# Query and key splits stacked by three transfers instead of row copies, with the four heads of a block side by side

## The chip, the cores and the metric

One Trainium2 chip, one of its cores. The metric is device time in microseconds of one execution of the whole program, lower is better. Profiles are single executions; line numbers such as L930 are lines of the kernel before.

## The reference

Input `x` has 8 batches of 512 tokens and 512 channels; a context of 77 tokens per batch has a length of its own per batch. Two residual steps follow each other, both with 16 heads of 32 channels:

```python
x = x + cross_attention(layernorm(x), ctx, ctx, valid_lens, Wq, Wk, Wv, Wo)   # keys past valid_lens masked
h = layernorm(x)
top_idx, gates = top_2(relu(mean(h) @ gw1.T + gb1) @ gw2.T + gb2)             # per batch, of 8 experts
q, k, v = (h @ (Wm + sum_k gate_k U_k S_k V_k).T + b for each of q, k, v)
x = x + self_attention(q, k, v) @ (Wm_o + ...).T + ob                         # softmax over 512 keys
```

Everything is float32. Scores are exponentiated after the row maximum is subtracted.

## The kernel before

The work of each batch `b` is cut into some 480 small steps (kinds such as `qk`, `sc`, `sT`, `pv`). A table, `CALENDAR`, gives each step of a batch a number, to which `b * PERIOD` is added; batches 0 and 7 and a few steps of batch 6 have numbers of their own in `OWN`. All steps are sorted by these numbers, and every engine, and SP's DMA queue, walks the sorted list and does the steps that are its own, in that order. The numbers have no other use: what counts is the order. Between engines, steps wait on semaphores. Six batches in the middle repeat one order, and neighbouring batches overlap: while batch 3 is in its self attention, batch 4 is in its cross attention.

Heads come in four jobs of four (`j`, or `i` in the cross attention): 128 columns of a projection hold four heads of 32 channels.

- `q1` and `qk` (through `product`, L1236) project a job's queries or keys into a bank of PSUM, 128 rows (head, channel) by 512 tokens, with float32 matmuls; each is recorded as two MATMULs. `out1`, `v` and `out2` are products of the same size.
- `q1_split`, `qk_split`: ScalarE writes the rounded high part to `stage_hi` (L898, L905), VectorE the remainder to `stage_lo` (L1048, L1055). There are three stage buffers. The float32r matmuls that follow take one pass each.
- The stack: a tile `qs`, `ks` or `qsc` of 32 rows per part, three parts on top of each other (high, high, low for queries; high, low, high for keys), the four heads side by side in columns, so that one matmul of 96 rows sums three products. Each of `qs` and `ks` has two slots (`j % 2`).
- `q1_rows`, `qk_rows`: ScalarE copies each head's 32 rows of `stage_hi` to part 0 of the stack: four ACTIVATE of 32 x 512 (L916, L930). `q1_stack`, `qk_stack`: SP issues four transfers of 64 KB from `stage_lo` to the low part (L692, L708), waits for the row copies, and issues one of 256 KB that copies part 0 to the other high part (L695, L711).
- `csc`, `sc` (L1282, L1293): scores, in two banks; VectorE takes the row maxima (L1064, L1072). `cross_shift`, `shift`: TensorE transposes the maxima (L1299), VectorE splits them (L1079, L1081), and `shift_move` (L747) moves them by two transfers of 8 KB into two more rows of the query stack. `csT`, `sT` (L1314, L1321): transposed scores with the maximum subtracted; ScalarE exponentiates them (L938, L949).
- `pv`, `den`, `cpv`, `cden`: four heads beside each other, eight MATMULs. `psum` (GpSimd) adds the exponentials over key tiles; `inv` takes reciprocals, `divide` scales.
- The gate of the next batch (`gate_hidden`, `gate_top`, `gate_scale`, `pick`, `uv_load`, `uv_hi`, `uv_lo`, `weff`) runs beside it: SP reads the chosen experts (`pick`) and loads their factors (`uv_load`) and the plain weights (`wm_load`, L727); `weff` (L1266) multiplies the factors, and VectorE adds the result to the plain weights (L1159).

The PSUM banks for products (`pj`, three) and the stage buffers are handed out in the sorted order, so the order also sets which step waits for which bank.

Of the kernel before, what the change touches and what calls it, by code (L numbers as in the profile page):

```python
# [16 lines left out]
H, DH = 16, 32  # L17
# [25 lines left out]
PERIOD = 32544  # L43
CALENDAR = {
    "context": (-29527,),
    "context_v": (-22528,),
    "load": (-32665,),
    "stats": (-32183, -31868, -31599, -31477),
    "deviation": (-30034, 295),
    "normalize": (-28685, 1275),  # L50
    "xpose": (-27589, -27427, -26822, -26780, 1562, 1957, 2590, 2902),
    "q1": (-26590, -26243, -25959, -25937, -26536, -25485, -24792, -24419, -18087, -17907, -17456, -16554, -12209,
        -12014, -11705, -11434),
    "q1_split": (-25157, -24232, -15571, -10200),
    "q1_rows": (-24756, -18383, -13331, -7974),
    "q1_stack": (-24276, -17659, -11767, -7302),
    "pick": (4904,),
    "uv_load": (5886, 6812, 9234, 43415),
    "csc": (-23802, -23433, -22705, -22506, -16659, -16588, -16069, -15948, -11709, -11333, -10125, -9654, -5344,
        -5090, -4931, -4819),  # L60
    "cross_shift": (-22083, -15813, -9063, -4218),
    "cross_shift_move": (-21652, -15771, -8769, -4153),
    "csT": (-20791, -20067, -19513, -19512, -14418, -14247, -13713, -13489, -8539, -8329, -8228, -8041, -3571, -3381,
        -3091, -3068),
    "cpv": (-18262, -10397, -6973, -2567),
    "cacc": (-18190, -10093, -6231, -2378),
# [12 lines left out]
    "uv_hi": (5956, 8589, 9867, 47462),
    "uv_lo": (6039, 8816, 10639, 49210),  # L80
    "weff": (6968, 7223, 8095, 8162, 9130, 9401, 9822, 9845, 10725, 10762, 12444, 12542, 53344, 53841, 53973, 55499),
    "qk": (8248, 8472, 8477, 8636, 9921, 10045, 10194, 10492, 17793, 18105, 19037, 19131, 19533, 19591, 19715, 19966,
        22679, 22995, 23492, 24077, 24628, 26820, 27705, 27722, 33581, 33788, 33991, 34872, 36496, 36571, 36871, 37170),
    "qk_split": (8792, 11460, 19921, 20217, 24193, 27804, 35667, 37980),
    "qk_rows": (12829, 12428, 21163, 21940, 28716, 28090, 37032, 38667),
    "qk_stack": (14166, 13070, 21170, 23206, 29374, 29180, 38577, 39510),
    "v": (11539, 12230, 12965, 13658, 12386, 12506, 12605, 14080, 14702, 15911, 16094, 16166, 16257, 16627, 16862,
        18707),
    "v_bias": (14155, 14210, 16179, 19056),
# [5 lines left out]
    "shift": (20612, 29950, 38368, 45601),  # L95
    "shift_move": (22291, 30030, 38966, 46828),
# [36 lines left out]
    "weff": {(7, 3, 0): 322347, (7, 3, 1): 329712, (7, 3, 2): 371975, (7, 3, 3): 389041, (0, 0, 0): 7543,
# [14 lines left out]
    "load": {(0,): -877946},  # L148
    "stats": {(0, 0): -446619, (0, 1): -446600, (0, 2): -446546, (0, 3): -435175},
# [180 lines left out]
def increments(step):  # L330
# [1098 lines left out]
```

## Time and profile before

| | |
|---|---|
| median of 3 runs | 1408.98 us (1406.68 to 1409.2) |
| the profiled execution | 1410.16 us, span of the trace 1408.4 us, TensorE clock 0.995 |
| TensorE matmuls | 1370.0 us busy (97%), 5704 instructions |
| weight loads | 690.0 us (49%) |
| VectorE, ScalarE, GpSimd | 948.3 us (67%), 857.2 us (61%), 679.7 us (48%) |
| DMA | 130.81 MB, mean 93 GB/s |

A row of the trace gives start and length of an instruction, or how often it came, and the idle time of its engine before it with the one that ended that. Ends of matmuls are modelled: several are in the pipeline at once, so rows overlap, and the length of one row is not the time that TensorE spends on it. The chain of waits shows what each added to the end.

### The profile page before, as it was taken

Reading aid. Unit: us, or ns where it says so; the run is one execution under the profiler, and the core shown is the slowest. Engines: PE = TensorE matmul, PEld = TensorE weight load, DVE = VectorE, ACT = ScalarE, POOL = GpSimd, SP = SyncE. Lnnn points to the kernel's source line nnn. Section 1 sums busy time; section 2 is a strip of 40 time slices with the busy share of each in tenths; the row PEclk is TensorE's granted clock in tenths of the full one; section 3 lists DMA queues with packets and bytes.
Section 4 is the critical chain, followed back from the end, with each engine's and each line's share of the span. In section 5 each row is a group of like instructions: output and inputs, shape, how many; then the busy total and the mean of one; then the engine's idle time right before and its main releaser. Section 6 shows DMA issues by size and latency. Waiting matters only on the chain.

```text
span 1408.4 us, 17104 instructions
## 1 busy us (share of the span) xinstructions
PE 1370.0 (97%) x5704; PEld 690.0 (49%) x5704; DVE 948.3 (67%) x1679; ACT 857.2 (61%) x1499; POOL 679.7 (48%) x411
## 2 busy tenths in 40 slices
PE   8999999999999999999999999999999999999987
PEld 5545445544455554554455544555544444444432
DVE  3573677767677776767677676767776667676573
ACT  2435566766488655866567654885558655585562
POOL 2023045554457543564556543575535545575485
PEclk9999999999999999999999999999999999999999
DMA  7443224423344213622244323442145222342311
GB/s 255 97 141 103 64 51 120 126 59 86 113 97 111 65 50 111 161 49 77 75 119 119 76 62 113 99 116 67 41 134 140 47 77 64 94 114 65 81 41 37
DMA packets 78767, 130.81 MB, mean 93 GB/s; under 512 B 26374, under 2 KB 32134, under 8 KB 75607
## 3 DMA queue, kind: packets, MB, share of 16 engines
q1 hardware_dynamic: 78103, 129.61, 34.6%
q8 instruction: 45, 0.74, 0.2%
q14 instruction: 43, 0.35, 0.1%
q10 hardware_dynamic: 576, 0.11, 0.1%
HBM read 66.08 MB, written 12.21 MB: 56 GB/s over the span
## 4 chain that ended last, share of the span: by engine, by line
PE 80%; ACT 5%; DVE 4%; DMA 4%; SPq 3%; issue 2%; POOL 1%; DVEq 0%; ACTq 0%; POOLq 0%
PE pj L1236 41%; PE scT L1321 8%; PE sc L1293 8%; PE acc L1350 7%; PE sc L1282 3%; PE pj L1266 2%; PE scT L1314 2%; PE pj L1338 2%; PE pj L1330 2%; PE pj L1359 1%; SPq L708 1%; PE pj L1209 1%; DVE inv_sum L1099 1%; DVE negmax L1072 1%; PE pj L1221 1%
## 5 line engine op out<-in xcount | busy, mean ns | idle before, releaser
L949 ACT ACTIVATE probs<-scT 128x512 f32<-128x512 f32 x512 | 289.5, 594 | 298.8 <-PE scT L1321 295.2
L1072 DVE TENSOR_REDUCE negmax<-sc 128x1 f32<-128x512 f32 x512 | 339.5, 681 | 151.1 <-PE sc L1293 148.3
L821 POOL TENSOR_TENSOR probs_sum<-probs_sum,probs 128x1024 f32<-128x1024 f32 x128 | 300.5, 2366 | 67.6 <-ACT probs L949 67.5
L1099 DVE RECIPROCAL inv_sum<-pj 128x128 f32<-128x128 f32 x256 | 225.7, 923 | 69.9 <-PE pj L1359 38.5
L817 POOL TENSOR_TENSOR probs_sum<-probs 128x1024 f32<-128x1024 f32 x64 | 151.2, 2369 | 247.7 <-ACT probs L949 247.7
L1321 PE MATMUL scT<-qs,ks 99*128 99x512 f32 x512 | 258.8, 541 | 10.4 <-DMA qs<-shift 5.3
L1293 PE MATMUL sc<-ks,qs 96*128 96x512 f32 x512 | 258.2, 532 | 3.5 <-DVE negmax L1072 1.8
L1236 PE MATMUL pj<-XT,Wqk 128*128 128x512 f32 x512 | 257.8, 595 | 0.0
L1321 PEld LDWEIGHTS scT<-qs,ks 99*128 99x128 f32 x512 | 94.0, 189 | 118.5 <-ACT probs L949 47.2
L1293 PEld LDWEIGHTS sc<-ks,qs 96*128 96x128 f32 x512 | 96.3, 189 | 111.3 <-issue 62.5
L1350 PE MATMUL acc<-probs,V 128*32 128x512 f32 x1024 | 132.2, 600 | 0.0
L1236 PE MATMUL pj<-Wvo,ctx2T 128*128 128x512 f32 x256 | 129.6, 598 | 0.2 <-DVE inv_sum L1099 0.2
L1236 PE MATMUL pj<-Wvo,XT 128*128 128x512 f32 x256 | 128.2, 599 | 0.2 <-DVE V L1170 0.2
L791 POOL TENSOR_TENSOR xhat<-xhat,inv_sum 128x128 f32<-128x128 f32 (+1 forms) x56 | 45.7, 820 | 170.6 <-DVE inv_sum L1099 116.6
L938 ACT ACTIVATE probs<-scT 77x512 f32<-77x512 f32 x128 | 71.2, 586 | 91.0 <-PE scT L1314 90.0
L1236 PE MATMUL pj<-XT,Wq_sb 128*128 128x512 f32 x256 | 126.2, 605 | 0.0
L1236 PE MATMUL pj<-Wo_sb,xhat 128*128 128x512 f32 x256 | 121.4, 596 | 0.0
L827 POOL TENSOR_TENSOR uv_stack<-UVS_sb,uv_stack 96x1024 fp32r<-96x1024 f32 x32 | 75.6, 2363 | 85.6 <-ACT UVS_sb L869 85.6
L1236 PEld LDWEIGHTS pj<-XT,Wqk 128*128 128x128 f32 x512 | 94.8, 190 | 45.2 <-issue 24.9
L1282 PEld LDWEIGHTS sc<-keys,qsc 97*128 97x128 f32 x480 | 69.6, 192 | 42.3 <-issue 28.3
L1282 PE MATMUL sc<-keys,qsc 97*128 97x78 f32 x480 | 82.8, 303 | 4.5 <-DMA qsc<-qsc 2.7
L1064 DVE TENSOR_REDUCE negmax<-sc 128x4 f32<-128x312 f32 x128 | 60.2, 475 | 33.1 <-PE sc L1282 32.9
(102 smaller groups left out, 1722.7 us busy)
## 6 DMA issues: line engine op xcount, KB each, us to landing
Wqk<-in_WmT SPq DMA_DIRECT2D x16, 1024.0 KB, 6.6
Wvo<-in_WmT SPq DMA_DIRECT2D x16, 1024.0 KB, 5.8
UVS_sb<-in_UVS SPq DMA_DIRECT2D x64, 192.8 KB, 3.2
qs<-stage_lo SPq DMA_DIRECT2D x136, 64.0 KB, 2.1
qs<-qs SPq DMA_DIRECT2D x34, 256.0 KB, 3.0
X<-in_x SPq DMA_DIRECT2D x8, 1024.0 KB, 8.1
ks<-stage_lo SPq DMA_DIRECT2D x128, 64.0 KB, 2.0
ks<-ks SPq DMA_DIRECT2D x32, 256.0 KB, 2.9
```

The costliest lines, as they stand in the source:

```text
L817: nc.gpsimd.tensor_tensor(probs_sum[:, pair], probs[:, 0, pair], probs[:, 1, pair], ALU.add)\
L821: nc.gpsimd.tensor_tensor(probs_sum[:, pair], probs_sum[:, pair], probs[:, kt % 2, pair], ALU.add)\
L827: nc.gpsimd.tensor_tensor(uv_stack[:].rearrange("p s n -> p (s n)"), UVS_sb[:, n, 0:2 * D], uv_stack[:].rearrange("p s n -> p (s n)").bitc ...
L938: nc.scalar.activation(probs1[0:NK, j, :], scT[0:NK, ST[step], :], ACT.Exp, scale=SCALE)\
L949: nc.scalar.activation(probs[:, kt % 2, jj, :], scT[:, ST[step], :], ACT.Exp, scale=SCALE)\
L1072: nc.vector.tensor_reduce(negmax[:, 0, n:n + 1], sc[:, SC[step], :], AX.X, ALU.max, negate=True)\
L1099: nc.vector.reciprocal(inv_sum[:, INV[use], at], pj[:, PJ[left_in(full)], at])\
L1236: mm = nc.tensor.matmul(pj[:, p, :], lhsT, rhs, start=(dc == 0), stop=(dc == DC - 1))
L1282: mm = nc.tensor.matmul(sc[:, SC[step], j * NKP:(j + 1) * NKP], cross_stack(b, i)[0:MASK_ROW + 1, j, t * P:(t + 1) * P], keys1[0:MASK_ROW ...
L1293: nc.tensor.matmul(sc[:, SC[step], :], qs[0:3 * DH, slot, jj, t * P:(t + 1) * P], ks[0:3 * DH, slot, jj, :], start=True, stop=True).then_i ...
L1321: nc.tensor.matmul(scT[:, ST[step], :], ks[0:ROWS, slot, jj, kt * P:(kt + 1) * P], qs[0:ROWS, slot, jj, :], start=True, stop=True).then_in ...
L1350: mm = nc.tensor.matmul(acc[jj * DH:(jj + 1) * DH, 0, :], V2[:, kt, v_slot(b, j), jj * DH:(jj + 1) * DH], probs[:, kt % 2, jj, :], start=( ...
```

## The change

The columns of the first query weight, and the output columns of the query and key weights and of their biases, are permuted on the host: within each block of 128, row `d * 4 + head` takes the place of row `head * 32 + d`. A split of 128 partitions by 512 is then, in order, 32 rows by four heads by 512, as the stack wants it. ScalarE's row copies are gone. SP issues three transfers of 256 KB per split, each from 128 rows of a stage buffer to 32 rows of the stack: two of the high part once ScalarE has written it, one of the low part once VectorE has. The waits that the row copies had (the slot is free, the constant rows are made) are SP's now. Nothing else in the computation changes; the numbers of all steps are new, in sixteenths of the old unit (520704 = 16 x 32544), those of batches 0 and 7 too.

```diff
-PERIOD = 32544
+PERIOD = 520704
 CALENDAR = {
-    "pick": (4904,),
-    "uv_load": (5886, 6812, 9234, 43415),
+    "pick": (69426,),
+    "uv_load": (76373, 89903, 137903, 683234),
...
-    "wm_load": (2594, 8306, -276, 53109),
+    "wm_load": (60219, 116462, 54068, 827809),
...
-    "gate_scale": (5530,),
+    "gate_scale": (80616,),
...
-    "qk_split": (8792, 11460, 19921, 20217, 24193, 27804, 35667, 37980),
-    "qk_rows": (12829, 12428, 21163, 21940, 28716, 28090, 37032, 38667),
-    "qk_stack": (14166, 13070, 21170, 23206, 29374, 29180, 38577, 39510),
...
-    "shift": (20612, 29950, 38368, 45601),
-    "shift_move": (22291, 30030, 38966, 46828),
...
+    "qk_stack": (212732, 185553, 342481, 374955, 491818, 480494, 603756, 608930),
...
+    "shift": (342227, 479168, 605178, 724794),
...
-    if kind in ("q1_rows", "qk_rows"):
-        return {"rows_copied": HJ}
     if kind == "q1_stack":
-        return {f"q1_stacked{home_of(*step[1:])}": 16 * (HJ + 1)}
+        return {f"q1_stacked{home_of(*step[1:])}": 16 * 3}
...
+            def stacked(stack, parts, n, split, done):
+                sp.wait_ge("stage_hi", sp.after("stage_hi", *split))
+                for part in parts[:2]:
+                    queue.dma_start(stack[part * DH:(part + 1) * DH].bitcast(F32), stage_hi[:, n, :].bitcast(F32))\
+                         .then_inc(done, 16)
+                sp.wait_ge("pj_left_by_dve", sp.after("pj_left_by_dve", *split))
+                queue.dma_start(stack[parts[2] * DH:(parts[2] + 1) * DH].bitcast(F32), stage_lo[:, n, :].bitcast(F32))\
+                     .then_inc(done, 16)
...
             def qk_stack(step, b, j, w):
                 split = "qk_split", b, j, w
-                n, slot = STAGE[split], slot_of(j)
-                stack, lo, hi = ((qs, 2, 1), (ks, 1, 2))[w]
-                sp.wait_ge("pj_left_by_dve", sp.after("pj_left_by_dve", *split))
+                slot, (stack, parts) = slot_of(j), ((qs, (0, 1, 2)), (ks, (0, 2, 1)))[w]
+                sp.wait_ge("consts_made", 7)
+                sp.wait_ge("ks_made", sp.after("ks_made", "key_rows", 1))
...
-                for jj in range(HJ):
-                    queue.dma_start(stack[lo * DH:(lo + 1) * DH, slot, jj, :].bitcast(F32),
-                                    stage_lo[jj * DH:(jj + 1) * DH, n, :].bitcast(F32)).then_inc(done, 16)
-                sp.wait_ge("rows_copied", sp.after("rows_copied", "qk_rows", b, j, w))
-                queue.dma_start(stack[hi * DH:(hi + 1) * DH, slot].bitcast(F32),
-                                stack[0:DH, slot].bitcast(F32)).then_inc(done, 16)
+                stacked(stack[:, slot], parts, STAGE[split], split, sems[f"{'qk'[w]}_stacked{slot}"])
...
-            def qk_rows(step, b, j, w):
-                slot, stack = slot_of(j), (qs, ks)[w]
...
-                for jj in range(HJ):
-                    nc.scalar.activation(stack[0:DH, slot, jj, :], stage_hi[jj * DH:(jj + 1) * DH, n, :].bitcast(F32),
-                                         ACT.Copy).then_inc(sems["rows_copied"], 1)
...
+    def by_row(a):
+        return np.asarray(a).reshape(*a.shape[:-1], DC, HJ, DH).swapaxes(-1, -2).reshape(a.shape)
```

In the new table `shift_move` has (346303, 481205, 606551, 734915), `qk_split` (126830, 171885, 314027, 318477, 394952, 472792, 569878, 607147).

## Rows read from the trace of the kernel before

**Rows 1.** Busy time by stretch: length, busy of each engine, clock, DMA share, GB/s.

```profile
0.00:220.00 220.00, 207.69 (x840) 112.01 (x840) 127.06 (x230) 103.31 (x175) 50.20 (x45) 0.98 0.43 123
220.00:1060.00 840.00, 833.67 (x3542) 424.01 (x3540) 597.22 (x1074) 546.69 (x963) 432.14 (x259) 1.00 0.36 92
1060.00:1240.00 180.00, 172.94 (x733) 85.40 (x732) 122.96 (x219) 115.67 (x205) 89.11 (x51) 1.00 0.33 85
1240.00:1408.40 168.40, 155.66 (x595) 68.57 (x593) 101.10 (x158) 91.56 (x160) 108.24 (x57) 0.99 0.24 65
```

**Rows 2.** Chain in order of time, 600 to 660 us: start, us, what.

```profile
608.91 1.72 PE pj L1236 x4
621.54 0.46 PE scT L1321 x2
624.20 0.37 PE sc L1282 x4
635.37 0.86 PE acc L1350 x8
```

**Rows 3.** Timeline of TensorE: the gate's matmuls of two neighbouring batches.

```profile
564.67 1.11 PE L1368 MATMUL pj<-pooled,gw1T_sb 128*128 128x128 f32 x8
728.04 1.12 PE L1368 MATMUL pj<-pooled,gw1T_sb 128*128 128x128 f32 x8
```

**Rows 4.** Groups of ScalarE by shape: count, busy us, mean ns, idle before.

```profile
L949 ACT ACTIVATE probs<-scT 128x512 f32<-128x512 f32 x512 | 289.5, 594 | 298.8 <-PE scT L1321 295.2 <-POOL probs_sum L817 1.3
L930 ACT ACTIVATE qs<-stage_hi 32x512 fp32r<-32x512 f32 x128 | 80.2, 627 | 2.7
```

**Rows 5.** Waits of TensorE's matmuls: us in total, times, longest.

```profile
PE scT L1321 <- DMA qs<-shift: 5.3, 8, 1.1
PE scT L1321 <- ACT probs L949: 3.4, 8, 0.5
...
PE sc L1282 <- DMA qsc<-qsc: 2.7, 2, 2.3
...
PE pj L1299 <- DVE stage_lo L1055: 1.6, 6, 0.3
```

**Rows 6.** Timeline, 731 to 762 us, around the end of job 2 of one batch.

```profile
733.23 2.58 ACT L930 ACTIVATE qs<-stage_hi 32x512 fp32r<-32x512 f32 x4
...
736.79 0.69 ACT L905 ACTIVATE stage_hi<-pj,qkb_sb 128x512 fp32r<-128x512 f32 x1
737.23 2.47 SPq L708 DMA_DIRECT2D qs<-stage_lo  x4
...
737.51 0.75 DVE L1055 SCALAR_TENSOR_TENSOR stage_lo<-pj,qkb_sb,stage_hi 128x512 fp32r<-128x512 f32 x1 [0.76 <-ACT stage_hi L905]
...
738.32 0.33 PE L1299 MATMUL pj<-ident_sb,negmax 128*128 128x128 f32 x1 [0.28 <-DVE stage_lo L1055]
...
740.38 1.23 SPq L747 DMA_DIRECT2D qs<-shift  x2
743.71 0.72 PE L1321 MATMUL scT<-qs,ks 99*128 99x512 f32 x2 [0.44 <-DMA qs<-shift]
...
752.98 0.58 SPq L727 DMA_DIRECT2D Wqk<-in_WmT  x1
...
760.00 1.28 DVE L1159 TENSOR_TENSOR Wqk<-pj,Wqk 128x512 f32<-128x512 f32 x2
```

**Rows 7.** DMA issues: count, KB each, us from issue to landing.

```profile
Wqk<-in_WmT SPq DMA_DIRECT2D x16, 1024.0 KB, 6.6
...
qs<-stage_lo SPq DMA_DIRECT2D x136, 64.0 KB, 2.1
qs<-qs SPq DMA_DIRECT2D x34, 256.0 KB, 3.0
...
ks<-ks SPq DMA_DIRECT2D x32, 256.0 KB, 2.9
...
qs<-shift SPq DMA_DIRECT2D x68, 8.0 KB, 2.4
```

More of the change, by code:

```diff
@@ new lines @@
+    "q1_stack": (-415245, -291066, -204261, -115894),
+    "pick": (69426,),
+    "uv_load": (76373, 89903, 137903, 683234),
+    "csc": (-399316, -392329, -386570, -361778, -279999, -267576, -262032, -259985, -181121, -174415, -153549,
+        -151999, -89000, -80879, -77224, -70003),
+    "cross_shift": (-357091, -258799, -145893, -61252),
+    "cross_shift_move": (-338882, -252460, -145637, -58247),
+    "csT": (-326112, -321104, -317390, -311544, -246868, -243436, -227048, -223831, -139203, -137355, -130085,
+        -128804, -42655, -42231, -39567, -39079),
@@ new lines @@
+    "cpv": (-282558, -158643, -117491, -36343),
+    "cacc": (-270843, -158024, -104649, -32670),
+    "cden": (-255862, -167520, -106954, -35308),
+    "cinv": (-253918, -250906, -245859, -223367, -163757, -161195, -160591, -155900, -104782, -84249, -77203, -76914,
+        -34463, -32438, -29645, -18601),
+    "wm_load": (60219, 116462, 54068, 827809),
+    "cdivide": (-161540, -148848, -47603, -28681, -11770, -8982, 1170),
+    "out1": (-50162, -44668, -40472, -14842, -27878, -27789, -23527, -9127, -9100, -6339, -2183, 5204, 3938, 6459,
+        6628, 10929),
@@ new lines @@
+    "residual1": (-8176, -1589, 9151, 13278),
+    "residual_bias": (298894,),
+    "token_sums": (32668, 44433, 48684, 49029),
+    "gate_hidden": (60147,),
+    "gate_top": (64114,),
+    "gate_scale": (80616,),
+    "uv_hi": (87261, 111461, 147491, 738169),
+    "uv_lo": (87300, 123017, 165328, 822345),
+    "weff": (101588, 107032, 109352, 111400, 128962, 137507, 140208, 147209, 174882, 175894, 178873, 189936, 850122,
+        864319, 867823, 898426),
+    "qk": (113828, 114593, 114952, 120109, 149163, 160907, 163385, 164241, 276060, 278903, 295107, 299779, 300581,
+        301097, 313751, 314218, 369736, 375334, 377029, 379567, 437349, 440750, 445804, 457938, 532516, 543784,
+        544129, 548328, 576496, 580646, 585989, 590801),
@@ new lines @@
+    "qk_split": (126830, 171885, 314027, 318477, 394952, 472792, 569878, 607147),
+    "qk_stack": (212732, 185553, 342481, 374955, 491818, 480494, 603756, 608930),
+    "v": (188740, 196964, 208643, 226468, 211931, 212863, 214459, 229455, 252723, 255436, 260811, 262576, 268470,
+        272012, 272014, 282674),
+    "v_bias": (229466, 234781, 264193, 287174),
[5 rows of a table added]
+    "shift": (342227, 479168, 605178, 724794),
+    "shift_move": (346303, 481205, 606551, 734915),
[7 rows of a table added]
+    "psum": (380589, 403679, 419958, 444044, 444527, 464186, 537796, 545354, 577378, 578721, 592602, 597747, 647186,
+        659111, 675085, 696260, 698722, 751132, 782551, 790720, 849174, 868486, 878058, 881981),
@@ new lines @@
+    "accout": (520658, 610322, 747005, 897008),
+    "den": (476400, 607559, 758606, 884123),
+    "inv": (476548, 479438, 480346, 481164, 612511, 612537, 613577, 614055, 761956, 763020, 777076, 782945, 889711,
+        894768, 901184, 902009),
+    "divide": (533142, 705594, 850295, 903864, 905126, 909312, 970769),
+    "out2": (902822, 903802, 906599, 916862, 913457, 914464, 916922, 917886, 938998, 939278, 949506, 957981, 967566,
+        971705, 976463, 989555),
+    "residual2": (918189, 918352, 959695, 989800),
@@ L207 @@
-    "gate_hidden": {(0,): 4930, (7,): 231575},
-    "gate_top": {(0,): 5490, (7,): 231738},
-    "gate_scale": {(0,): 5710, (7,): 232050},
-    "pick": {(0,): 5670, (7,): 232919},
-    "warm": {(0, 2): -96451, (1, 3): -47401, (2, 1): -40402, (3, 4): -29966, (4, 5): -24131, (5, 2): -3041,
-        (6, 3): 3898, (7, 3): 4589, (8, 2): 8768, (9, 3): 9592, (10, 4): 11483},
-    "residual_bias": {(7,): 242974},
[7 rows of a table removed]
-    "qk_split": {(7, 0, 0): 236698, (7, 0, 1): 238528, (7, 1, 0): 248314, (7, 1, 1): 249344, (7, 2, 0): 267927,
-        (7, 2, 1): 266852, (7, 3, 0): 310186, (7, 3, 1): 321828},
@@ new lines @@
+    "context": {(0,): -4192709},
+    "context_v": {(0,): -1151284, (7,): 3296262},
+    "wm_load": {(7, 3): 5049208, (0, 0): -555476, (0, 1): -545137, (0, 2): 127050, (7, 1): 3743833, (7, 0): 3684340,
+        (7, 2): 3648630},
+    "uv_load": {(7, 3): 3873399, (0, 0): 85489, (0, 1): 104189, (0, 2): 122536, (7, 2): 3738706, (7, 0): 3705733,
+        (7, 1): 3726657},
+    "uv_hi": {(7, 3): 4774211, (0, 0): 87401, (0, 1): 113882, (0, 2): 157228, (7, 1): 3740283, (7, 2): 3791436,
+        (7, 0): 3721389},
@@ new lines @@
+    "uv_lo": {(7, 3): 5310646, (0, 0): 98804, (0, 1): 118690, (0, 2): 176485, (7, 1): 3764726, (7, 2): 3818370,
+        (7, 0): 3732600},
+    "weff": {(7, 3, 0): 5311761, (7, 3, 1): 5312059, (7, 3, 2): 5445882, (7, 3, 3): 6767537, (0, 0, 0): 99661,
[14 rows of a table added]
+    "load": {(0,): -15904755},
+    "stats": {(0, 0): -15845340, (0, 1): -15844419, (0, 2): -15838204, (0, 3): -9167904},
+    "deviation": {(0, 0): -9159449, (0, 1): 16037, (7, 1): 3652060},
+    "normalize": {(0, 0): -6602126, (0, 1): 19582, (7, 1): 3671415},
@@ new lines @@
+    "csT": {(0, 0, 0): -1199395, (0, 0, 1): -1199186, (0, 0, 2): -1181853, (0, 0, 3): -1180673, (0, 1, 0): -1132007,
[5 rows of a table added]
+    "cpv": {(0, 0): -1142434, (0, 1): -732056, (0, 2): -648967, (0, 3): -80188, (7, 0): 3392474, (7, 1): 3445833,
+        (7, 2): 3528428, (7, 3): 3609282},
+    "cacc": {(0, 0): -1121586, (0, 1): -720649, (0, 2): -83537, (0, 3): -79327, (7, 0): 3393471, (7, 1): 3448477,
+        (7, 2): 3533095, (7, 3): 3609477},
+    "cden": {(0, 0): -1148189, (0, 1): -1046493, (0, 2): -664387, (0, 3): -544673, (7, 0): 3389423, (7, 1): 3473974,
+        (7, 2): 3537267, (7, 3): 3611764},
@@ new lines @@
+    "cinv": {(0, 0, 0): -1132201, (0, 0, 1): -1129012, (0, 0, 2): -1117869, (0, 0, 3): -736503, (0, 1, 0): -727355,
[6 rows of a table added]
+    "cdivide": {(0, 0, 0): -718118, (0, 1, 0): -583452, (0, 2, 0): -80738, (0, 3, 0): -78635, (0, 3, 1): -64755,
[11 rows of a table added]
+    "token_sums": {(0, 0): 49688, (0, 1): 65308, (0, 2): 68626, (0, 3): 68706, (7, 0): 3676931, (7, 1): 3686265,
+        (7, 2): 3686524, (7, 3): 3691101},
+    "gate_hidden": {(0,): 68746, (7,): 3695798},
+    "gate_top": {(0,): 74895, (7,): 3696637},
+    "gate_scale": {(0,): 76550, (7,): 3699359},
@@ new lines @@
+    "pick": {(0,): 76841, (7,): 3700382},
+    "warm": {(0, 2): -4194136, (1, 3): -3603782, (2, 1): -3595382, (3, 4): -1057802, (4, 5): 55759, (5, 2): 68223,
+        (6, 3): 68968, (7, 3): 89527, (8, 2): 129061, (9, 3): 171381, (10, 4): 406600},
+    "residual_bias": {(7,): 3736107},
[8 rows of a table added]
+    "qk_split": {(7, 0, 0): 3759505, (7, 0, 1): 3829138, (7, 1, 0): 3976891, (7, 1, 1): 3989439, (7, 2, 0): 4414129,
+        (7, 2, 1): 4411404, (7, 3, 0): 5117183, (7, 3, 1): 5438284},
+    "qk_stack": {(7, 0, 0): 3823567, (7, 0, 1): 3841901, (7, 1, 0): 4006334, (7, 1, 1): 4027510, (7, 2, 0): 4467432,
[5 rows of a table added]
@@ new lines @@
+    "v_bias": {(7, 0): 3873002, (7, 1): 3874231, (7, 2): 3909227, (7, 3): 3957891},
[13 rows of a table added]
+    "shift": {(7, 0): 3981117, (7, 1): 4452327, (7, 2): 5310973, (7, 3): 6705351},
+    "shift_move": {(7, 0): 4007764, (7, 1): 4468990, (7, 2): 5313784, (7, 3): 6745515},
[20 rows of a table added]
+    "psum": {(7, 0, 1, 0): 4128274, (7, 0, 1, 1): 4409351, (7, 0, 2, 0): 4427773, (7, 0, 2, 1): 4432218,
[5 rows of a table added]
+    "accout": {(7, 0): 4813425, (7, 1): 5440670, (7, 2): 6823813, (7, 3): 14056979},
+    "den": {(7, 0): 4765132, (7, 1): 5446756, (7, 2): 6820617, (7, 3): 14053237},
@@ L290 @@
            "normalize": product(PAIR), "xpose": product(PAIR, FOUR), "q1": product(JOBS, FOUR),
-           "q1_split": product(JOBS), "q1_rows": product(JOBS), "q1_stack": product(JOBS),
+           "q1_split": product(JOBS), "q1_stack": product(JOBS),
            "pick": [()], "uv_load": product(FOUR), "csc": product(JOBS, FOUR), "cross_shift": product(JOBS),
@@ L297 @@
            "weff": product(FOUR, FOUR), "qk": product(JOBS, PAIR, FOUR), "qk_split": product(JOBS, PAIR),
-           "qk_rows": product(JOBS, PAIR), "qk_stack": product(JOBS, PAIR), "v": product(FOUR, FOUR),
+           "qk_stack": product(JOBS, PAIR), "v": product(FOUR, FOUR),
            "v_bias": product(FOUR), "sc": product(JOBS, range(TT * HJ)), "shift": product(JOBS),
@@ L906, in qk_split @@
                                      bias=qkb_sb[:, w, j:j + 1]).then_inc(sems["stage_hi"], 1)
-            def q1_rows(step, b, i):
-                before = home_before(b, i)
-                act.wait_ge("consts_made", 7)
-                if before:
-                    act.wait_ge("scoresT_full", act.after("scoresT_full", "csT", *before, HJ - 1))
-                act.wait_ge("stage_hi", act.after("stage_hi", "q1_split", b, i))
-                n = STAGE["q1_split", b, i]
-                for j in range(HJ):
-                    nc.scalar.activation(cross_stack(b, i)[0:DH, j, :], stage_hi[j * DH:(j + 1) * DH, n, :].bitcast(F32), ACT.Copy)\
-                        .then_inc(sems["rows_copied"], 1)
-            def qk_rows(step, b, j, w):
-                slot, stack = slot_of(j), (qs, ks)[w]
-                before = (b, j - 2) if j >= 2 else (b - 1, j + DC - 2)
-                act.wait_ge("consts_made", 7)
-                act.wait_ge("ks_made", act.after("ks_made", "key_rows", 1))
-                if b == 0 and w == 0 and j < 2:
-                    act.wait_ge("scoresT_full", act.after("scoresT_full", "csT", 0, j + 1, HJ - 1))
-                act.wait_ge("scoresT_full", act.after("scoresT_full", "sT", *before, TT - 1, HJ - 1))
-                act.wait_ge("stage_hi", act.after("stage_hi", "qk_split", b, j, w))
-                n = STAGE["qk_split", b, j, w]
-                for jj in range(HJ):
-                    nc.scalar.activation(stack[0:DH, slot, jj, :], stage_hi[jj * DH:(jj + 1) * DH, n, :].bitcast(F32),
-                                         ACT.Copy).then_inc(sems["rows_copied"], 1)
             def csT(step, b, i, j):
@@ L1400 @@
     keypos[:, :NK] = np.arange(NK)
+    def by_row(a):
+        return np.asarray(a).reshape(*a.shape[:-1], DC, HJ, DH).swapaxes(-1, -2).reshape(a.shape)
+    for p in "qk":
+        w[p + "Wm"], w[p + "U"], w[p + "b"] = by_row(w[p + "Wm"].T).T, by_row(w[p + "U"].transpose(0, 2, 1)).transpose(0, 2, 1), by_row(w[p + "b"])
     ins = {
```

145 lines of the change are left out of this document (33 added, 112 removed), and 225 rows, old and new, of tables (CALENDAR, OWN).

## Prediction

> **What bounds the kernel now.** I read the busy time by stretch first. TensorE's matmuls are busy for 833.67 of the 840 us in the middle, at clock 1.00; its idle time is 12.3 us in the first 220, 6.3 in the middle, 7.1 up to 1240 and 12.7 at the end [rows 1]: 38.4 us in all. ScalarE is 65% busy in the middle and VectorE 71%. The rows overlap, so I asked the chain of waits what a matmul adds to the end: four products cost 1.72 us, so 0.43 each, two single-pass matmuls of 512 columns 0.46, four cross scores 0.37, and eight matmuls of `pv` side by side 0.86 [rows 2].
>
> With these prices one batch is: 96 products of two MATMULs, 192 x 0.43 = 82.6 us; 64 `sc`, 64 `sT`, 16 `csT` and 16 `weff`, 160 x 0.23 = 36.8; 28 groups of eight (16 `pv`, 4 each of `den`, `cpv`, `cden`), 28 x 0.86 = 24.1; 16 `csc` of 0.37 = 5.9; transposes and gate, about 5.5 by the same reading. That is 155 us. The gate's matmuls of neighbouring batches are 728.04 - 564.67 = 163.4 us apart [rows 3]. So a batch in the middle loses some 8.5 us (5%) to switches between kinds of matmul and to waits, and six batches some 50 us. No change of order can give back more than this, and the switches are in any order. The change touches no matmul: kinds, shapes and numbers are the same, so TensorE's 155 us per batch stay.
>
> What does ScalarE cost TensorE today? Its exponentials stand idle for 298.8 us, 295.2 of it waiting for TensorE [rows 4]: in most places ScalarE is early. TensorE's matmuls wait 3.4 us in total for an exponential, 2.7 us for the stack of `qsc`, and 5.3 us in eight places for the moved maxima, `qs<-shift`; the transpose before that waits 1.6 us in six places for a remainder `stage_lo` [rows 5].
>
> **The change part by part.**
>
> *The row copies.* 32 splits of cross attention and 64 of self attention, four copies each: 384 x 0.627 = 240.8 us of ScalarE's 857.2 disappear [rows 4]. Worth on TensorE: only where a copy stands in a chain that TensorE waits for. The timeline shows one that comes back each batch, at the end of job 2. ScalarE copies four rows from 733.23 to 735.81; behind them it transposes out, and writes `stage_hi` of the next job at 736.79; VectorE has idled 0.76 us for that and does the remainder at 737.51; the transpose of the maxima, which wants the bank freed by this remainder, starts at 738.32 after 0.28 us idle [rows 6]. SP meanwhile issues four transfers in 2.47 us from 737.23 and the fifth after them, so the maxima are moved only at 740.38, and `sT` starts at 743.71 after 0.44 us idle [rows 6]. In the new table three things differ here. `qk_split` of that job (607147) stands behind `shift` (605178), where it stood before it (37980 and 38368). `uv_load` of the next batch, 520704 + 76373 = 597077, and the `qk_stack` that SP does next (603756) are ahead of `shift`; the old ones, 38430 and 38577, were behind. And that stack is three issues, not five. So the maxima need not queue. In the trace, the eight and six waits of these two kinds sum to 6.9 us [rows 5], plus some 0.2 us each of pipeline that runs dry before the row calls it idle (a transpose is listed 0.33 us long, but eight gate matmuls of the same size take 1.11 together [rows 3]): 14 x 0.2 = 2.8. Bounds: nothing, and 9.7 us. I take two thirds, **-6 us**, since the order between `shift` and `sT` is as long as before (`pv`, `den` and three products of `q1`, 5 x 0.86 = 4.3 us in both tables).
>
> *The stack's own latency.* Before, after `stage_hi`: 2.58 us of copies, then one 256 KB transfer, 2.9 to 3.0: 5.5 us, the low parts beside it. After: two issues at once and a third when the remainder is there (0.75 us later, hidden). An issue costs SP 2.47 / 4 = 0.62 us [rows 6], so the third leaves after 1.24 us. A 64 KB transfer lands after 2.0 to 2.1 us and a 256 KB one after 2.9 to 3.0 [rows 7]; the 0.9 us between them is 192 KB of data, so 256 KB is 1.2 us. Three of them share the engines: 1.2 to 1.8 us until data flow, 3.6 us of data, 0.5 for the end, 5.3 to 5.9 us. Were 128 short rows cheaper than 32 long ones, 4.2 (issue-bound). The chain is as long as it was or 1.3 us shorter, and needs no ScalarE. TensorE's wait for a stack is 2.7 us, 2.3 of it in one place [rows 5]; I take half, **-1.4**, bounds 0 and -2.7. In the new order of a middle batch 8.5 us or more of matmuls lie between what frees a stack, or its last product, and its first score, so 5.9 is covered; without this cover it would be up to 0.4 us for each of 96.
>
> *Exponentials.* ScalarE 28% emptier lets `sT` find its bank free: 3.4 us of waits [rows 5] are all there is; **-1.5**, bounds 0 and -3.4.
>
> *DMA.* 96 splits move 768 KB instead of 512: 25.2 MB more in all, and 96 x (3.6 - 4 x 0.3 - 1.2) = 115 us more of the engines' time, where their share is 0.24 to 0.43 [rows 1]. Behind a stack in SP's list is `shift_move`: in the new order each of the four sits right behind a stack. Its 2.4 us [rows 7] can grow by the stack's last transfer, 1.2 us. Against that SP is free 1.2 us sooner (two issues fewer). Net **+1**, bounds 0 and +16 (below).
>
> Here the Trainium skill, "DMA: Bandwidth & Descriptors", Rules for kernel authors, speaks against the change: two transfers to disjoint partition groups do not run beside each other, they serialise on the same 16 engines. The trace does not show three of 256 KB together; its single ones are in line with the data rate assumed above. By the rule the three take 3.6 us of data, by the issue bound 2.9 would do.
>
> *The key weights.* Their plain part is loaded right behind a `q1_stack`: issued at 752.98, landed 6.6 us later [rows 7], and VectorE adds to it at 760.00 [rows 6], just in time. New: SP gets there two issues (1.2 us) earlier and without the remainder's place to wait for, some 2.8 us sooner in sum; the stack's data ahead are 1.2 us longer; and the first `weff` of the keys stands 2.2 us of matmuls earlier in the order. That is 0.6 us late: 7 x 0.6, against VectorE's other work in front; **+1**, bounds 0 and +4.
>
> *SP's waits.* A `qk_stack` now waits on SP for `stage_hi` and for its slot; before it waited for the remainder, the slot and the copies. Behind it wait `shift_move`, `uv_load` and stores as before. No cost: remainder and copies ended later than `stage_hi`.
>
> *The order elsewhere.* Sorted by the new numbers, TensorE's list of a middle batch has the same neighbours in about the same numbers, products behind products 29 times instead of 26, `pv` groups behind each other 7 instead of 6. A `sc` behind products or behind itself costs nothing over its price, a group of eight behind a single-pass matmul about 0.1 us by the starts in the timeline. I take **-1**, bounds -5 and +5. One gap shrinks: between `gate_hidden` and `gate_top` 4.2 us of matmuls stood, now 0.7, about what ScalarE's one ACTIVATE between them needs; **+1** for seven batches. Start and end: the same chains in nearly the same order; 0, bounds -8 and +8.
>
> Sum: -6 - 1.4 - 1.5 + 1 + 1 - 1 + 1 = **-6.9 us** on a profiled execution of 1410.16 us (span 1408.4), so 1403.3; against the median of the runs, 1408.98, that is **1402 us** (-0.5%).
>
> **The rivals.** A measurement of this kernel tells about 0.2% (2.8 us) from no change.
>
> *No change.* The copies ran while ScalarE would have waited for TensorE anyway [rows 4], and the 8.5 us per batch are switches. For it: single waits are short [rows 5]. Against it: job 2's wait returns each batch. 1406 to 1411 us, chance 0.19.
>
> *Slower, by the shift behind the stack.* The place is `sT` of each job. Without a queue the move needs 0.3 (VectorE) + 0.6 (the first issue) + 0.6 + 2.4 (the second, from issue to landing) = 3.9 us, and 4.3 to 6.5 us of matmuls stand between `shift` and `sT`. It decides when the stack adds over 0.6 us in job 2. If the three transfers, once started, hold the queue for 3.6 us and the move comes right behind them, it is late by up to 2 us in job 2 and by 0.5 us in the three others: 8 x 2 + 24 x 0.5 = 28 us, less the 9 us of the other terms: 1420 to 1428. Against it: SP has two issues fewer, and `shift` often comes after the stack's data. Together with an order that loses on its own (+5, start and end +8), chance 0.22.
>
> *A larger gain.* A freer ScalarE and the new order shrink start and end as well, where TensorE idles 12.3 + 7.1 + 12.7 = 32.1 us [rows 1]; a third of it and all waits of rows 5 (13 us) give some -7 - 11 - 4 = -22, or 1387 us, range 1383 to 1395. The Trainium skill, "Perfetto Trace Analysis", Identifying the Most-Contended Engine, says that matmul busy time is a poor measure and weight loads' busy share a better one; that is 49% here, and would leave more room. The 155 of 163.4 us speak against it in the middle. Chance 0.17.
>
> **How the numbers follow.** Forecast (1395 to 1406): chance 0.42. Faster than 1406: 0.42 + 0.17 = 0.59; the same 0.19; slower 0.22. The bounds -5 of the order and -8 of start and end reach 1389 from the forecast, those of the opposite sign, +5 and +8, 1415; with part of the larger gain the range is 1387 to 1416, leaving out some 0.07 below and 0.12 above.
>
> **What would show it.** Right: no row of L930 or L916, ScalarE near 617 us, DMA near 156 MB, the wait for `qs<-shift` and for `stage_lo` below 3 us together, the pitch of the gate's matmuls near 162.4 us. Wrong: `qs<-shift` landing later than 3 us and more TensorE waits on it; TensorE waiting for the stacks, if three transfers take over 7 us; a pitch that is the same, with waits under other names.

## The result and the profile after

The changed kernel takes **1526.7 us** (median of four runs, 1525.1 to 1533.6) beside 1407.8 us for the kernel before on the same chip: ratio **1.085**, 95% interval 1.082 to 1.089. The prediction was 1402 us, faster with chance 0.59, range 1387 to 1416. It was wrong in sign, and the time lies far outside the range. The profiled execution has a span of 1523.3 us; the rows below are from it.

Busy time by stretch in the columns of [rows 1] (length, then TensorE's matmuls, weight loads, VectorE, ScalarE, GpSimd, granted clock, DMA share, GB/s): four stretches, and then 3 us windows early in the run.

```profile
0.00:220.00 220.00, 201.93 (x787) 111.24 (x788) 118.58 (x219) 65.76 (x112) 47.32 (x40) 0.95 0.60 127
220.00:1120.00 900.00, 843.88 (x3510) 424.80 (x3509) 588.50 (x1046) 398.08 (x706) 423.09 (x255) 0.98 0.59 104
1120.00:1310.00 190.00, 180.63 (x742) 90.19 (x740) 123.95 (x227) 85.17 (x151) 89.80 (x54) 0.98 0.55 98
1310.00:1523.30 213.30, 182.73 (x670) 79.37 (x668) 116.04 (x189) 83.41 (x150) 120.06 (x63) 0.94 0.41 75
...
183.00:186.00 3.00, 3.00 (x22) 1.02 (x20) 2.31 (x5) 0.60 (x1) 0.00 (x0) 1.00 1.05 127
186.00:189.00 3.00, 0.65 (x4) 0.56 (x4) 2.67 (x4) 0.71 (x2) 0.19 (x1) 1.00 1.06 126
189.00:192.00 3.00, 3.00 (x13) 1.87 (x12) 0.93 (x2) 1.57 (x3) 1.09 (x1) 0.66 1.01 119
192.00:195.00 3.00, 3.00 (x10) 1.67 (x8) 1.13 (x3) 1.08 (x2) 0.00 (x0) 0.77 0.02 3
...
231.00:234.00 3.00, 3.00 (x9) 1.51 (x8) 0.30 (x1) 2.08 (x4) 1.28 (x1) 1.00 1.08 353
```

The middle now needs 900 us where it needed 840. TensorE is idle for 56 us of it (6.3 before), and the DMA share has gone from 0.36 to 0.59. The windows show why that share deserves a second look: while stacks move, all 16 engines count as busy (1.05) and carry 126 GB/s; while a weight is loaded from memory (231 to 234) they count just as busy and carry 353.

The gate's matmuls of two neighbouring batches, as in [rows 3]:

```profile
607.29 1.07 PE L1343 MATMUL pj<-pooled,gw1T_sb 128*128 128x128 f32 x8
...
785.32 1.06 PE L1343 MATMUL pj<-pooled,gw1T_sb 128*128 128x128 f32 x8
```

They are 178.0 us apart; before, 163.4. What TensorE's matmuls wait for (total, times, longest), beside [rows 5]:

```profile
PE scT L1296 <- DMA qs<-shift: 35.3, 21, 3.3
PE sc L1268 <- DMA qs<-stage_lo: 24.1, 7, 4.0
PE sc L1257 <- DMA qsc<-stage_lo: 14.7, 16, 1.4
PE sc L1268 <- DMA ks<-stage_lo: 11.0, 8, 4.0
```

Together 85.1 us. Before, the same four made 9.0: 5.3 for `qs<-shift`, 2.7 for the stack of `qsc`, nothing for that of `qs`, and for that of `ks`

```profile
PE sc L1293 <- DMA ks<-ks: 1.0, 2, 0.6
```

Transfers from issue to landing (count, KB each, median us), beside [rows 7]:

```profile
qs<-stage_hi SPq DMA_DIRECT2D x68, 256.0 KB, 6.2
...
qs<-stage_lo SPq DMA_DIRECT2D x34, 256.0 KB, 8.1
...
qs<-shift SPq DMA_DIRECT2D x68, 8.0 KB, 5.8
```

The 8 KB move of the maxima takes 5.8 us instead of 2.4. The chain of waits shows one such place (start, us, what):

```profile
172.82 0.61 SPq L690
...
174.13 7.05 DMA qsc<-stage_lo
...
181.23 0.64 PE sc L1257 x4
...
183.87 4.43 DMA qs<-shift
...
188.35 0.73 PE scT L1296 x2
```

The three transfers of this stack, issued 0.65 us apart from 172.82 on:

```profile
DMA to landing us min/median/max: 4.3/5.7/7.1
```

So they land 2.0 to 2.1 us apart, which is also 256 KB at the 126 to 127 GB/s of the windows, and from the first issue to the last landing (181.18) the stack takes 8.4 us. A second stack is issued right behind it; the last line gives KB and the time from issue to landing of its third transfer:

```profile
174.93 1.20 SPq L690 DMA_DIRECT2D qs<-stage_hi  x2
...
178.08 0.55 SPq L693 DMA_DIRECT2D qs<-stage_lo  x1
```

```profile
qs<-stage_lo SPq DMA_DIRECT2D x1, 256.0 KB, 9.3
```

It is complete at 187.4, 12.5 us after its first issue. The maxima, sent at 183.25 and 183.87, land behind it, at 187.8 and 188.3. TensorE does 0.65 us of work in 186 to 189. Behind that idle stretch the granted clock is 0.66 and 0.77 for two windows: part of them at 1.2 instead of 2.4 GHz.

The sum: idle time of TensorE 1523.3 - 1409.2 = 114.1 us, before 38.4, so +75.7, about what the four waits grew by (76). Its busy time grew by 39.2 us for the same 5704 matmuls, while the mean granted clock fell from 0.995 to 0.972; by those two clocks alone 1370.0 us would become 1402 (an estimate), 32 of the 39.

### The profile page after: what moved, and what is told of

Its sections match the earlier page's. It is cut to its first block, busy times and chain, and to the rows that moved or that the text cites. A ratio compares the mean times of both kernels' runs of the same rounds, so it can differ in the third digit from the quotient of the medians.

```text
span 1523.3 us, 16576 instructions
## 1 busy us (share of the span) xinstructions
PE 1409.2 (93%) x5704; PEld 705.6 (46%) x5704; DVE 947.1 (62%) x1679; ACT 632.4 (42%) x1115; POOL 680.3 (45%) x411
## 2 busy tenths in 40 slices
DMA packets 97194, 155.92 MB, mean 102 GB/s; under 512 B 23302, under 2 KB 29062, under 8 KB 97111
## 4 chain that ended last, share of the span: by engine, by line
PE 61%; DMA 24%; DVE 5%; SPq 3%; ACT 2%; issue 2%; POOL 1%; DVEq 0%; ACTq 0%; POOLq 0%
PE pj L1211 32%; DMA qsc<-stage_lo 9%; PE sc L1268 6%; PE scT L1296 6%; DMA qs<-shift 6%; DMA ks<-stage_lo 5%; DMA qs<-stage_lo 3%; PE acc L1325 3%; PE sc L1257 3%; SPq L690 2%; PE pj L1241 2%; PE scT L1289 1%; PE pj L1184 1%; DVE negmax L1047 1%; PE pj L1205 1%
## 5 line engine op out<-in xcount | busy, mean ns | idle before, releaser
L1296 PE MATMUL scT<-qs,ks 99*128 99x512 f32 x512 | 272.4, 565 | 38.4 <-DMA qs<-shift 35.3
L1211 PE MATMUL pj<-Wvo,XT 128*128 128x512 f32 x256 | 135.3, 631 | 0.0
L1211 PE MATMUL pj<-XT,Wq_sb 128*128 128x512 f32 x256 | 133.5, 628 | 0.0
L1325 PE MATMUL acc<-probs,V 128*32 128x512 f32 x1024 | 129.0, 603 | 0.0
L1257 PE MATMUL sc<-keys,qsc 97*128 97x78 f32 x480 | 73.2, 286 | 17.8 <-DMA qsc<-stage_lo 14.7
```

The source lines that it names most:

```text
L1211: mm = nc.tensor.matmul(pj[:, p, :], lhsT, rhs, start=(dc == 0), stop=(dc == DC - 1))
L1257: mm = nc.tensor.matmul(sc[:, SC[step], j * NKP:(j + 1) * NKP], cross_stack(b, i)[0:MASK_ROW + 1, j, t * P:(t + 1) * P], keys1[0:MASK_ROW ...
L1296: nc.tensor.matmul(scT[:, ST[step], :], ks[0:ROWS, slot, jj, kt * P:(kt + 1) * P], qs[0:ROWS, slot, jj, :], start=True, stop=True).then_in ...
L1325: mm = nc.tensor.matmul(acc[jj * DH:(jj + 1) * DH, 0, :], V2[:, kt, v_slot(b, j), jj * DH:(jj + 1) * DH], probs[:, kt % 2, jj, :], start=( ...
```

## The experiments

Theories at the outset: **A**, a transfer from 128 rows into 32 adjacent rows is slow because of where it lands; **B**, it is slow because it comes in 2 KB pieces; **C**, the transfers are harmless and the new places of the steps lose the time.

**1. The transfers alone (`probe`).** Its core, with `src` of 128 x 512, `src4` of 128 x 4 x 512, `dst` of 128 x 4 x 512; each call waits for its landing:

```python
narrow_64(dst[32:64, 0, :], src[0:32]);  narrow_256(dst[32:64], src4[0:32])
narrow_gaps(wide[32:64, :, 0:S], src4[0:32])            # four pieces of 2 KB per row
stack_32(dst[0:32], src[:]);  stack_step3(dst[0:96:3], src[:]);  stack_step4(dst[0:128:4], src[:])
rows_128(flat[:], src[:]);  rows_64(dst[0:64, 0:2, :], src[:])
# then three in a row: adjacent rows, rows 3 apart, rows 4 apart
```

> Nothing of the layer is computed here: the output is zeros, and SBUF to SBUF transfers alone run, one after the other, three times round. In the changed kernel a 256 KB stack transfer (128 source rows of 2 KB into 32 adjacent destination rows of 8 KB) that starts on an idle queue lands after 4.2 to 4.3 us, and three in a row land 2.06 us apart. Theory A (it is slow because it lands in 32 adjacent destination rows): the same 256 KB into rows 3 apart or 4 apart, or into 128 rows, lands at least 0.7 us earlier than into 32 adjacent rows, and three in a row come at 1.2 us or less each. Theory B (it is slow because it comes in 2 KB pieces from 128 source rows): all of these land within 0.3 us of one another, three in a row 2.06 us apart in every spread. Both: 64 KB from 32 rows to 32 rows lands near 2.3 us, 256 KB from 32 rows of 8 KB near 3.0 us.

DMA issues of the first round in this order, one window for each (KB, us to landing):

```profile
dst<-src SPq DMA_DIRECT2D x1, 64.0 KB, 2.0
...
dst<-src SPq DMA_DIRECT2D x1, 256.0 KB, 2.8
...
wide<-src SPq DMA_DIRECT2D x1, 256.0 KB, 3.0
...
dst<-src SPq DMA_DIRECT2D x1, 256.0 KB, 4.0
...
dst<-src SPq DMA_DIRECT2D x1, 256.0 KB, 2.9
...
dst<-src SPq DMA_DIRECT2D x1, 256.0 KB, 2.3
...
flat<-src SPq DMA_DIRECT2D x1, 256.0 KB, 2.3
...
dst<-src SPq DMA_DIRECT2D x1, 256.0 KB, 3.8
```

And the three in a row, first the adjacent rows, then 3 apart, then 4 apart (issues 0.6 us apart):

```profile
DMA to landing us min/median/max: 4.2/5.6/6.8
...
DMA to landing us min/median/max: 3.0/3.7/4.1
...
DMA to landing us min/median/max: 2.3/2.4/2.5
```

The same 256 KB from the same 128 rows take 4.0 us into 32 adjacent rows, 2.9 into rows 3 apart, 2.3 into rows 4 apart or 128 rows. Pieces of 2 KB cost only 0.2 us (3.0 against 2.8), so B falls. In a row they land about 1.9, 1.2 and 0.7 us apart (the differences of these rows plus the distance of the issues; 0.7 is hardly more than that distance). 64 adjacent rows (3.8) are hardly better than 32: it is not the number of rows. Nor is it the landing place alone: 32 adjacent rows take the same 256 KB from 32 rows in 2.8 us. Slow is the pair, 128 rows into adjacent rows; with this limit A stands so far.

**2. Which spread counts (`probe2`).** As before, with `dst[0:64:2]` (rows 2 apart), 64 rows to 64 rows, and 32 long rows into 128 rows.

> Zeros are put out and transfers alone run, three times round. In the probe before, 256 KB from 128 rows landed after 3.95 us on 32 adjacent rows, 3.83 us on 64 adjacent rows, 2.88 us on 32 rows 3 apart, 2.32 us on 32 rows 4 apart and 2.29 us on 128 rows. Now 32 rows 2 apart. Theory A1 (what counts is the span of destination rows): between 1 apart and 3 apart, 3.2 to 3.6 us, three in a row some 1.5 to 1.7 us apart. Theory A2 (what counts is how many of the memory's ports the rows reach that are written at one time, as the 64 adjacent rows hint, which span 64 rows and gained nothing): 3.8 to 4.0 us, three in a row 2 us apart. 256 KB from 64 rows to 64 rows: 2.8 to 3.1 us, from 32 rows of 8 KB into 128 rows of 2 KB: 2.3 to 4.0 us.

Adjacent, 2 apart, and 32 long rows into 128:

```profile
dst<-src SPq DMA_DIRECT2D x1, 256.0 KB, 4.0
...
dst<-src SPq DMA_DIRECT2D x1, 256.0 KB, 3.9
...
flat<-src SPq DMA_DIRECT2D x1, 256.0 KB, 3.6
```

Rows 2 apart span twice as many partitions and gain 0.1 us; three in a row land after 4.1, 5.6 and 6.6 us, as on adjacent rows (64 rows to 64 rows: 2.9 us, as expected). So A1 (the span) falls. A2 (which rows are written at one time) fits, but no view shows which rows these are.

**3. The stack on rows 3 apart (`n_interleave3`).** Row `d` of part `p` lies on partition `3d + p`, in the stacks and in the context's keys; a sum over the rows doesn't care for their order.

```diff
-                    queue.dma_start(stack[part * DH:(part + 1) * DH].bitcast(F32), stage_hi[:, n, :].bitcast(F32))\
+                    queue.dma_start(stack[part:3 * DH:3].bitcast(F32), stage_hi[:, n, :].bitcast(F32))\
...
-                queue.dma_start(stack[parts[2] * DH:(parts[2] + 1) * DH].bitcast(F32), stage_lo[:, n, :].bitcast(F32))\
+                queue.dma_start(stack[parts[2]:3 * DH:3].bitcast(F32), stage_lo[:, n, :].bitcast(F32))\
...
-                    queue.dma_start(keys1[part * DH:(part + 1) * DH].bitcast(F32),
+                    queue.dma_start(keys1[part:3 * DH:3].bitcast(F32),
```

> The changed kernel, with row d of part p of a stack (and of the context's keys) on destination partition 3d+p in place of 32p+d; all else as it is, the sums over the rows of a stack are the same. Theory A (adjacent destination rows make the transfers slow): stack transfers at 1.2 us or less each, the waits of TensorE for stacks and shift rows (86 us in the changed kernel) fall to 25 us or less, and the time to 1385 to 1430 us. Theory B (2 KB pieces): no difference, 1515 to 1540 us. Theory C (the new order of the steps): within 20 us of the changed kernel.

**1392.9 us** (1391.3 to 1393.3): 134 us less than the changed kernel by this alone (141 by the two ratios: the kernel before takes 1407.8 to 1411.6 us on the chips used, so a difference between two runs is good to some 7 us), and ratio 0.986 (0.982 to 0.989) to the kernel before. It beats both. Its DMA issues, gate and waits:

```profile
qs<-stage_hi SPq DMA_DIRECT2D x68, 256.0 KB, 3.8
...
qs<-stage_lo SPq DMA_DIRECT2D x34, 256.0 KB, 4.9
...
qs<-shift SPq DMA_DIRECT2D x68, 8.0 KB, 2.6
```

```profile
554.69 1.07 PE L1343 MATMUL pj<-pooled,gw1T_sb 128*128 128x128 f32 x8
...
716.92 1.06 PE L1343 MATMUL pj<-pooled,gw1T_sb 128*128 128x128 f32 x8
```

```profile
PE scT L1296 <- ACT probs L924: 3.1, 8, 0.5
PE scT L1296 <- DMA qs<-shift: 3.0, 4, 0.8
```

The wait for the maxima is 3.0 us, that for stacks is gone from the list, the pitch is 162.2 us, TensorE is busy 98% of 1391.5 us at clock 0.996. The slow transfers are the cause of the loss.

**4. Places and stacking taken apart (`n_old_stack`, `o_new_stack`, `o_interleave3`).** `n_old_stack` has the new places and the old stacking; the row copies, which have no place in the new table, stand right behind the last step that they wait for, a choice of mine. The two `o_` kernels have the old table without the row copies, with the changed stacking, and with it on rows 3 apart. The edits, in outline:

```diff
 # n_old_stack: the code of before, the new table, and for each split
+    q1_rows, qk_rows = right behind the latest of its split, the last csT or sT of the stack's slot, key_rows
 # o_new_stack (code of after), o_interleave3 (code of experiment 3)
-PERIOD = 520704
+PERIOD = 32544
+CALENDAR, OWN = those of before, less q1_rows and qk_rows
```

> The new places of all steps kept, but the stacking done as in the kernel before: four row copies by ScalarE, four 64 KB transfers and one of 256 KB, with the row copies put in right behind the last step that they must wait for. Theories A and B (the transfers lose the time): 1400 to 1440 us, since ScalarE has its 96 x 2.4 us of row copies again in an order that left them no room. Theory C (the new places lose it): 1480 us or more.

> The places of the kernel before kept, with the changed stacking: three 256 KB transfers and no row copies. Theories A and B (the transfers lose the time): 1470 to 1560 us. Theory C (the new places lose it): 1390 to 1415 us, near the forecast of 1402 us.

> The places of the kernel before, with the changed stacking on rows 3 apart: the fast stacks without the new order. If the new order is worth nothing by itself (the prediction's -1 us, within 5): 1388 to 1400 us. If the new order is what makes the three transfers fit: 1405 to 1450 us.

| medians, us | row copies by ScalarE | three transfers, adjacent rows | three transfers, rows 3 apart |
|---|---|---|---|
| old places | 1407.8 to 1411.6 (before) | 1577.3 | 1410.1 |
| new places | 1463.8 | 1526.7 (after) | **1392.9** |

C falls as the cause of the loss: the slow transfers lose more in the old places (ratio 1.116, 1.110 to 1.122) than in the new. Each of the three runs corrected me in something. 1577 is above the 1560 that A allowed. `n_old_stack` is 24 us above its 1440, between what A and B allowed and what C did, and slower than the kernel before; its two longest waits, 30 of TensorE's 71 us of idle time, are for what ScalarE brings late,

```profile
PE pj L1143 <- POOL uv_stack L704: 16.5, 8, 2.5
PE pj L1107 <- ACT XT L758: 13.5, 7, 2.2
```

the transposes `XT` and, over `uv_hi`, the expert factors; where I put the copies may have part in it. And `o_interleave3` is level with the kernel before (ratio 1.000, 0.998 to 1.002). Taking the copies off ScalarE is worth nothing there on balance: the wait for the shift rows (the moved maxima) is 13.2 us longer than the 5.3 us of [rows 5],

```profile
PE scT L1164 <- DMA qs<-shift: 18.5, 11, 2.8
```

and the rest of TensorE's idle time is 7.9 us shorter (in the profiled executions 1412.3 - 1368.6 - 18.5 = 25.2, before 38.4 - 5.3 = 33.1). Its gate's matmuls:

```profile
561.28 1.11 PE L1211 MATMUL pj<-pooled,gw1T_sb 128*128 128x128 f32 x8
...
726.08 1.11 PE L1211 MATMUL pj<-pooled,gw1T_sb 128*128 128x128 f32 x8
```

**5. Only the stacks of self attention spread (`n_inter_self`).**

```diff
+            def rows(part, apart):
+                return slice(part, 3 * DH, 3) if apart else slice(part * DH, (part + 1) * DH)
...
+                apart = split[0] == "qk_split"
...
+                    queue.dma_start(stack[rows(part, apart)].bitcast(F32), stage_hi[:, n, :].bitcast(F32))\
```

> The changed kernel with rows 3 apart only in the stacks of self-attention; those of cross-attention (32 of the 96 stacks) stay on adjacent rows. If the loss goes by the waits of TensorE seen for the cross stacks (14.7 of 86 us) it is 1410 to 1425 us; if each slow stack costs alike (a third of 134 us) it is 1430 to 1445 us.

1427.1 us (1424.8 to 1436.8): 34 us more than with all stacks spread (39 by the ratios) for the 32 slow stacks of cross attention and the context's keys, which also stay on adjacent rows; so 100 for the 64 of self attention. It lies between the two expectations, nearer to that by the waits. The wait that is left is the same as in the changed kernel (13.4 us beside 14.7):

```profile
PE sc L1261 <- DMA qsc<-stage_lo: 13.4, 14, 1.5
```

**6. The shift rows on another queue (`n_shift_act`, `n_interleave3_act`).** Is it SP's one queue that makes the maxima late? Their two transfers go to ScalarE's queue, at the same places of the order.

```diff
             def move_shift(side, dst, done, b, turn):
-                    sp.wait_ge(split, sp.after(split, *turn))
+                    act.wait_ge(split, act.after(split, *turn))
...
-            sp.walk({..., "shift_move": shift_move, "cross_shift_move": cross_shift_move})
+            act.walk({"shift_move": shift_move, "cross_shift_move": cross_shift_move, ...})
```

> The changed kernel with its slow stacks, but the shift rows' two transfers issued from ScalarE's queue, at the same places of the order. Theory D (the shift rows wait their turn behind stack transfers on one queue): the 35.3 us of TensorE's wait for them go, with what hangs on it: 1465 to 1500 us. Theory E (the stacks' own landing is what is late, and the shift rows share the same engines of transfer whatever their queue): 1510 to 1540 us.

> The kernel with all stacks on rows 3 apart (1392.9 us), with the shift rows' transfers issued from ScalarE's queue as in the run that rose to 1646 us. If that run rose because ScalarE's own queue is a bad place for them (128 issues of 0.57 us in the order of the exponentials, which then stand behind waits for VectorE): it rises by as much here, 1470 us or more. If it rose because small transfers wait for the packets of slow stacks whichever queue they are in, and because SyncE, no longer held at the shift rows, put the next stacks ahead of them: within 25 us of 1392.9 us here.

With slow stacks 1646.2 us, 120 us worse than the changed kernel; D and E both miss. The maxima land later, not earlier (7.7 us, 5.8 on SP's queue), and TensorE waits three times as long:

```profile
qs<-shift ACTq DMA_DIRECT2D x68, 8.0 KB, 7.7
```

```profile
PE scT L1295 <- DMA qs<-shift: 105.3, 27, 7.8
```

Another queue did not make the small transfers land sooner here. In the changed kernel SP's queue also stood still behind `shift` before it sent the maxima, and held the next stacks back with them (its waits there):

```profile
SPq L747 <- DVE shift L1054: 394.6, 64, 25.5
```

In `n_shift_act` SP has no such wait. With fast stacks the same edit costs 23.8 us (1416.7; 25 by the ratios, at the edge of the 25 allowed), and TensorE waits 10.4 us for the maxima where it waited 3.0:

```profile
PE scT L1295 <- DMA qs<-shift: 10.4, 11, 1.6
```

So some 24 us of the 120 come with ScalarE's queue as such, and the larger part only with slow stacks. Whether that part is more packets ahead of the maxima, or stacks that SP sends sooner, is not settled.

## Why the prediction was wrong

**The step that failed is the size of the stack's data time**: "the 0.9 us between them is 192 KB of data, so 256 KB is 1.2 us". The rows behind it [rows 7] are transfers from 32 rows to 32 rows; I took them over to 128 rows into 32 without a bound on the slow side, and bounded only the fast side (4.2 us). Measured, such a transfer takes 2.07 us (256 KB at 126.5 GB/s; 1.9 apart in the probe) and not 1.2. Three make 6.2 us instead of 3.6; the stack above takes 8.4 us, not 5.3 to 5.9; the six transfers of two stacks on each other's heels need 12.4. The prediction had named two signs of this: maxima landing later than 3 us (5.8), and TensorE waiting for stacks when three transfers take over 7 us. (The 2.9 us that it sets beside the 3.6 us of data is a landing time; its own 4.2 us, less 1.2 to 1.8 and 0.5, leave 1.9 to 2.5. Nothing rests on it.)

What rests on that number fell with it. "5.9 is covered" by 8.5 us of matmuls: at 8.4 us the cover is used up, at 12.5 behind another stack it is far too short, and the waits for stacks are 49.8 us, where I had a gain of 1.4. The shift behind the stack was costed at +1 with a bound of +16, and its rival at 28 us by a queue held for 3.6 us. The mechanism of that rival is what the chain shows, and 35.3 us of waits are its direct price; but at 1420 to 1428 us it was sized by the same 1.2 us. The clock, which fell to 0.66 behind the idle stretch shown above, was in no term: some 32 us by the estimate above.

With the data time that I had assumed the kernel gains: on rows 3 apart three transfers land about 1.2 us apart (experiment 1) and it takes 1392.9 us, inside the range. This does not confirm the sum, though: the gain is 18.7 us on that chip, where the sum had 6.9. "The row copies, -6" joined two things, a freer ScalarE and the new places of the steps. No run frees ScalarE and leaves all else, so its own worth stays open; in the old places, whatever it is, the longer wait for the maxima takes it back (experiment 4). It is the new places that keep the maxima from queueing, as that paragraph worked out from the table: with fast stacks they take that wait from 18.5 to 3.0 us, and they are worth 17 us (1410.1 to 1392.9; 20 by the ratios), where "the order elsewhere" had -1 and the two terms together -7. By the gate's matmuls a batch takes 164.8 us in `o_interleave3` and 162.2 with the new places (predicted: 162.4); six times 2.6 is 15 of these 17. Right were 155.92 MB and the missing rows of L930 and L916; ScalarE is 632.4 us busy, 617 expected.

Why adjacent rows are slow is explained, not shown: no view here lists which engine wrote which row. The Trainium skill, "SBUF — State Buffer", Door 1: The DMA port swizzle, says that the rate goes by how many of 16 ports the partitions reach, with rows 0 to 31 on eight of them and rows 0 to 63 on the same eight. The Trainium skill, "DMA: Bandwidth & Descriptors", The descriptor swizzle, says that on a transfer to 128 partitions each engine writes partitions in groups of four. Put together for this shape (my step, engines following the source rows), destination rows 0 to 7 and 16 to 23 are written first, four ports of 16; rows 2 apart reach four at a time as well, rows 4 apart all 16. By the 27 GB/s a port that the Trainium skill gives in that section on the port swizzle, four ports make 109 GB/s, an estimate. The kernel shows 126 to 127, so the picture is not exact, and the measurement decides. The order of the probes agrees with it: 2 apart no better than adjacent, 64 adjacent rows no better than 32, 4 apart as good as 128 rows.

## What to carry to other kernels

A rate is taken over from a row only if its shape on both sides is the same: source rows, destination rows, and how far apart. Where a transfer changes shape, bound its time from the slow side too, and work out what is late if that bound is true; here a factor of 1.7 on one number turned a gain of 1.4% into a loss of 8.5%. When a stack's rows may stand in any order, try orders that spread each transfer over the partitions, and measure them: 2 apart gained 0.1 us here, 3 apart 1.1, and 4 apart (1.7) was tried alone, not in the kernel. And plan the places of the steps for the transfers that there are.

## What the runs showed of the hardware

- A 256 KB transfer within the on-chip memory from 128 rows lands after 4.0 us on 32 adjacent rows, 3.9 on rows 2 apart, 2.9 on rows 3 apart, 2.3 on rows 4 apart and on 128 rows; from 32 rows of 8 KB into 32 rows 2.8, into 128 rows 3.6. Three in a row from 128 rows land about 1.9 us apart on adjacent rows, 1.2 on rows 3 apart.
- The DMA share is 1.05 at 126 GB/s and 1.08 at 353 GB/s: the share alone does not tell how fast data move.
- 8 KB sent from ScalarE's queue landed later (7.7 us) than from SP's queue behind the same kind of stacks (5.8 us).
